# Edge coefficients of a graph kernel: from sixteen wide GpSimd operations to thirty-two narrow VectorE operations a tile

## The chip, the cores and the metric

The kernel runs on 1 core of one Trainium2 chip. The metric is the device time of one execution in microseconds; the profiled execution is one such run, with its trace.

## What is computed

A graph of 3125 nodes with 128 features and 103125 edges, sorted by destination. First comes a relational layer with 8 relations that share 4 bases, then two transformer layers over the same edges with 2 heads, each part with a residual and a norm:

```python
Hb = einsum('ni,bio->bno', h, V)            # 4 bases
coef = w_comp[etype]                        # (edges, 4)
m = sum_b coef[:, b] * Hb[b][src]           # then times norm (the edge weight)
agg = segment_sum(m, dst)
hn = relu(agg + h @ loop_w + bias)
y = hn @ ffn_w.T + ffn_b + h                # then layer norm, residual, norm
x = transformer_conv(relu(transformer_conv(x, ...)), ...)   # q, k, v, softmax over the edges of a node
```

The change is about `coef * norm`: for each edge, four numbers, each the sum over the 8 relations of (weight if the edge is of relation r, else 0) times `w_comp[r, b]`.

## The kernel before

`message` computes the relational layer in 25 tiles of 125 destination nodes; `conv`, called twice, computes the transformer layers over dense 125 x 3125 score tiles with an additive mask (`bias`) that `message` writes to memory.

In `message` each of the 128 partitions is a destination node with 64 edge slots. For tile s, GpSimd fetches the edge data (`find_row`, `find_slots`: indirect DMAs); VectorE makes `kinds` (L682, partition x 8 relations x 64 slots: the weight where the type is r, else 0) and `digits` in `slot_kinds`; the coefficients go to `codes` (4 bases x 2 copies x 64 slots); TensorE transposes `digits` (L832) and `codes` (L840) and ScalarE copies them out (`digitsT` L1011, `weightsT` L1023). VectorE then builds one-hot matrices in 8 units a tile (`build_hot`: `Hw` L735, `L` L737, `Hw` L740) in a ring of 4 buffers, TensorE multiplies them (L857, `pair_products`, side 0 is units 0 to 3, side 1 units 4 to 7), ScalarE copies the products out (`MT` L962), and TensorE sums them with the node features (L869, `sums`). Four times a tile TensorE also transposes counts (L880, `turn_counts`), ScalarE takes their logarithm (L989, `logs`), and VectorE turns that into the mask (L756, `bias_row`), which SyncE stores.

Each engine runs its own list of steps t, written out by hand, with semaphores between engines. At step t VectorE works on several tiles: `first(t-5)`, `second`, `third` (norms), `build_hot(t-3, 4..7)`, `search(t)`, `search_row(t-1)`, `bias_row(t-4, 0..3)`, `build_hot(t-2, 0..3)`, `slot_kinds(t-1)`. In `step` of VectorE the loop variable k runs over 8 slots: k = 0 holds `first` and the build of unit 4, k = 1 `search` and unit 5, k = 2 `second`, `search_row`, unit 6 and `bias_row(u, 0)`, k = 3 unit 7 and `bias_row(u, 1)`, `bias_row(u, 2)`, k = 7 `slot_kinds`. Three waits matter: the build of a unit waits until the unit whose buffer it takes is multiplied (L732, unit 4 waits for unit 0); `logs(u, 2)` waits for `bias_row(u, 0)` (L988, two buffers); and TensorE's `turn_counts(u, 3)` waits for `logs(u, 2)` (`read`, L886), `turn_codes` for `logs(u, 3)`, which waits for `bias_row(u, 1)`.

The coefficients are made on GpSimd in `coefs`, at the head of its step t for tile t-2: for each base one multiply of 512 columns by the broadcast coefficients (L577), then adds of 256, 128 and 128 columns (L578 to L580). For tile 0 alone VectorE makes three of the four bases (`first_tile`, L716 to L719), with `slot_kinds(0)` after the first of them. `root` (L558), the inverse square roots of the norms, is on GpSimd also.

At the head of each `conv`, TensorE projects q and k in 7 chunks of up to 500 columns (L1498, L1499) and ScalarE copies both out with their bias (L1611, L1614).

Of the kernel before, what the change touches and what calls it, by code (L numbers as in the profile page):

```python
# [16 lines left out]
F32 = mybir.dt.float32  # L17
# [13 lines left out]
SLOTS = 64  # L31
# [40 lines left out]
def is_int(t):  # L72
    return isinstance(t, int)
# [387 lines left out]
def message(nc, a, m):  # L461
# [5 lines left out]
    with ctx:  # L467
        def sb(name, shape, dt):
            return ctx.enter_context(nc.sbuf_tensor(name, shape, dt))

        def sem(name):
# [19 lines left out]
        part, part_v = sb("coef_parts", [128, RELS, SLOTS], F32), sb("coef_parts_v", [128, RELS, SLOTS], F32)  # L491
# [33 lines left out]
         asked2, rooted2, nrm1, nrm2, lifted, s3, kinds_ok, blank_ok, turned_ps, turned_ok, first_v, first_ok, first_kinds, digits_ps, digitsT_ok) = (  # L525
# [5 lines left out]
                "first_v", "first_ok", "first_kinds", "digits_ps", "digitsT_ok"))  # L531
# [19 lines left out]
        def _(pool):  # L551
# [9 lines left out]
            def coefs(s, par, halfway):  # L561

                first = is_int(s) and s == 0
                then = Steps(pool, gps, 0 if first else s * COEF_STEPS - (COEF_STEPS - FIRST_COEF_STEPS))
                to = codes[par]
                if is_int(s) and s == 0:
                    pool.wait_ge(m["comp_in"], 16)
                if not is_int(s) or s >= 2:
                    pool.wait_ge(codes_ps, s - 1)
                if first:  # L570
                    pool.wait_ge(first_kinds, 1)
                else:
                    pool.wait_ge(kinds_ok, s + 1)
                bases = BASES - FIRST_ON_V if first else BASES
                for b in range(bases):
                    c = comp[:, :].rearrange("p (r b) -> p b r", b=BASES)[:, b, :].unsqueeze(2).to_broadcast([128, RELS, SLOTS])
                    then(nc.gpsimd.tensor_tensor(part[:, :, :], kinds[:, :, :], c, ALU.mult))  # L577
                    then(nc.gpsimd.tensor_tensor(part[:, 0:4, :], part[:, 0:4, :], part[:, 4:8, :], ALU.add))  # L578
                    then(nc.gpsimd.tensor_tensor(part[:, 0:2, :], part[:, 0:2, :], part[:, 2:4, :], ALU.add))
                    last = nc.gpsimd.tensor_tensor(to[:, b, :, :], twice(part[:, 0, :]), twice(part[:, 1, :]), ALU.add)  # L580
                    if b < bases - 1:
                        then(last)
                    if b == 1:
                        halfway()
                last.then_inc(codes_ok, 1)
                pool.wait_ge(codes_ok, s + 1)

# [20 lines left out]
            def step(t, par):  # L608
                def first_root():
                    if inside(t - 5):  # L610
                        root(t - 5, 1 - par, 0)

                if inside(t - 2):
                    coefs(t - 2, par, first_root)
                else:
                    first_root()
                if inside(t - 5):
                    root(t - 5, 1 - par, 1)
                if inside(t - 4):
                    lift(t - 4, par)  # L620
                if inside(t) and (not is_int(t) or t >= EARLY):
                    if not is_int(t) or t >= 2:
                        pool.wait_ge(slot_ok, t - 1)
                    find_row(nc, pool, a, m, t, par)
                if is_int(t) and t == 1:
                    for s in range(EARLY):
                        find_slots(s, s)
                if inside(t - 1) and (not is_int(t) or t > EARLY):
                    find_slots(t - 1, 1 - par)
# [29 lines left out]
        def _(v):  # L659
# [25 lines left out]
            def slot_kinds(s, par):  # L685
# [5 lines left out]
                if not first:  # L691
                    v.wait_ge(kind_in[par], (half(s, par) + 1) * 32)
                V.tensor_scalar(off[:, :], e_dst[par][:, :], node[par][:, :], OWN, ALU.is_equal, ALU.mult)
# [11 lines left out]

            def first_tile():

                then = Steps(v, first_v)
                to = codes[0]
                v.wait_ge(kind_in[0], 32)  # L710
                kinds_of(0).then_inc(first_kinds, 1)
                v.wait_ge(m["comp_in"], 16)
                v.wait_ge(first_kinds, 1)
                for b in range(BASES - FIRST_ON_V, BASES):
                    c = comp[:, :].rearrange("p (r b) -> p b r", b=BASES)[:, b, :].unsqueeze(2).to_broadcast([128, RELS, SLOTS])
                    then(V.tensor_tensor(part_v[:, :, :], kinds[:, :, :], c, ALU.mult))  # L716
                    then(V.tensor_tensor(part_v[:, 0:4, :], part_v[:, 0:4, :], part_v[:, 4:8, :], ALU.add))
                    then(V.tensor_tensor(part_v[:, 0:2, :], part_v[:, 0:2, :], part_v[:, 2:4, :], ALU.add))
                    last = V.tensor_tensor(to[:, b, :, :], twice(part_v[:, 0, :]), twice(part_v[:, 1, :]), ALU.add)  # L719
                    if b < BASES - 1:  # L720
                        then(last)
                    if b == BASES - FIRST_ON_V:
                        slot_kinds(0, 0)
                last.then_inc(first_ok, 1)
# [101 lines left out]
        def _(pe):  # L826
# [8 lines left out]
            def turn_codes(s, par):  # L835
                pe.wait_ge(codes_ok, s + 1)
                if s == 0:
                    pe.wait_ge(first_ok, 1)
# [513 lines left out]
def conv(nc, a, m, layer, out):  # L1352
# [4 lines left out]
    with ctx:  # L1357
# [35 lines left out]
        names = ("dve", "q_ps", "q_ok", "k_ok", "v_ps", "v_ok", "qk", "masked", "neg_ok", "exp_ok", "t_ps", "pa_ok",  # L1393
# [13 lines left out]
        EXP_AT = 3  # L1407
        block = ctx.enter_context(nc.Block())
# [27 lines left out]
        def buffer_free(eng, u, i):  # L1436

            if not is_int(u) or u >= 1:
                eng.wait_ge(z["pv_ok"], (u - 1) * CH + (i // HEADS + 1))

# [49 lines left out]
        def _(pe):  # L1490
            pe.wait_ge(z["one"], 1)

            def project(j):

                if j >= 2:
                    pe.wait_ge(z["q_ok"], j - 1)
                    pe.wait_ge(z["k_ok"], j - 1)
# [24 lines left out]
            def scores(t, par, n):  # L1522
# [3 lines left out]
                if is_int(t) and t == 0:  # L1526
                    pe.wait_ge(z["k_ok"], j + 1)
# [258 lines left out]
```

## Time and profile before

| what | before |
|---|---|
| median of 3 runs | 1973.23 us (1972.51 to 1973.4) |
| profiled execution, device time | 1973.07 us |
| its span, first to last instruction | 1971.1 us |
| `message` in it | about 0 to 1057 us |
| TensorE, VectorE, ScalarE, GpSimd busy | 96%, 74%, 65%, 34% |
| mean granted TensorE clock | 0.994 |

The span plus 1.97 us around it is the device time. Times in timelines are microseconds from the start of the span. Busy time of an engine is the union of its instructions; where neighbouring instructions overlap in the pipeline, a row of x8 shows the union and not eight durations.

### The profile page before, as it was taken

The numbers are of one execution on the slowest core, as the hardware profiler recorded it, in microseconds if no ns is written. First come the engines' busy times: TensorE is split into PE (matmuls) and PEld (weight loads), VectorE is DVE, ScalarE is ACT, GpSimd is POOL, SyncE is SP. The second block draws the span as 40 slices with busy tenths as digits, with TensorE's granted clock in tenths as the row PEclk, the third lists the DMA queues.
The fourth block names the chain that finished last, engine by engine and source line by source line (L and its number), as shares of the span: only waits on it lengthen the run. The fifth ranks groups of instructions, "written<-read, shape, count | busy, mean of one in ns | idle before, by whom it ended". The sixth has DMA issues, their size and how long they took to land. (4 is left out here: it accounts for less than half of the span.)

```text
span 1971.1 us, 53480 instructions
## 1 busy us (share of the span) xinstructions
PE 1899.6 (96%) x19165; PEld 1647.1 (84%) x19165; DVE 1449.5 (74%) x4127; ACT 1281.2 (65%) x2289; POOL 673.3 (34%) x802
## 2 busy tenths in 40 slices
PE   1999999999999999999998999999999999999998
PEld 0889999999999999999995788888887788888887
DVE  5988878887888788778744777677663777777775
ACT  0757766777677767676764666666665666666665
POOL 3775676567656765676400000000000000000000
PEclk9999999999999999999998999999999999999999
DMA  3012111211111111111103222222211233222230
GB/s 78 15 49 70 41 41 50 70 41 41 52 68 41 41 54 66 40 41 53 60 35 131 101 100 97 80 85 96 97 65 66 101 107 106 98 93 92 103 105 11
DMA packets 43018, 137.00 MB, mean 70 GB/s; under 512 B 9190, under 2 KB 24359, under 8 KB 36484
## 3 DMA queue, kind: packets, MB, share of 16 engines
q1 hardware_dynamic: 38484, 128.24, 18.1%
q0 software_dynamic: 4400, 6.80, 1.5%
q8 instruction: 104, 1.70, 0.4%
q14 instruction: 30, 0.25, 0.0%
HBM read 91.83 MB, written 43.20 MB: 69 GB/s over the span
## 5 line engine op out<-in xcount | busy, mean ns | idle before, releaser
L869 PE MATMUL ps<-matrixT,x_rows 125*128 125x256 f32 (+1 forms) x2500 | 563.5, 377 | 0.1
L869 PEld LDWEIGHTS ps<-matrixT,x_rows 125*128 125x128 f32 x2500 | 461.3, 190 | 48.4 <-issue 0.2
L1729 DVE CUSTOM_DVE_ANT_0 scores_l<-ps,bias_rows_l 125x500 f32<-125x500 f32 (+1 forms) x700 | 390.0, 619 | 29.5 <-issue 28.6
L962 ACT COPY matrixT<-ps 125x500 f32<-125x500 f32 (+2 forms) x800 | 381.6, 659 | 38.4 <-PE ps L857 38.3
L857 PEld LDWEIGHTS ps<-high_weights,low_onehot 64*125 64x125 f32 x6300 | 355.0, 188 | 20.4 <-issue 17.2
L857 PE MATMUL ps<-high_weights,low_onehot 64*125 64x125 f32 x6300 | 364.9, 273 | 7.3 <-DVE high_weights L740 7.3
L1630 ACT ACTIVATE scores_l<-scores_l,neg_max_l 125x1500 f32<-125x1500 f32 x200 | 317.3, 1600 | 7.3 <-DVE neg_max_l L1750 7.3
L1518 PEld LDWEIGHTS ps<-weightsT_l,values_l 125*64 125x64 f32 x5000 | 267.8, 136 | 36.4 <-issue 34.1
L1559 PE MATMUL ps<-eye,scores_l 125*125 125x125 f32 x2500 | 295.2, 275 | 0.0
L1559 PEld LDWEIGHTS ps<-eye,scores_l 125*125 125x125 f32 x2500 | 281.1, 189 | 10.1 <-issue 9.5
L1541 PE MATMUL ps<-kT_l,q_tile_l 64*125 64x500 f32 (+1 forms) x1400 | 287.2, 547 | 1.7 <-issue 1.6
L1518 PE MATMUL ps<-weightsT_l,values_l 125*64 125x125 f32 x5000 | 279.7, 270 | 1.6 <-ACT hT L1658 1.6
L1638 ACT COPY weightsT_l<-ps 125x500 f32<-125x500 f32 x400 | 220.4, 577 | 91.9 <-PE ps L1559 86.9
L737 DVE TENSOR_TENSOR low_onehot<-own_low,digitsT 128x1000 f32<-128x1000 f32 x200 | 279.8, 1399 | 0.0
L1737 DVE COPY weightsT_l<-ps 125x500 f32<-125x500 f32 x200 | 135.1, 677 | 159.5 <-PE ps L1559 159.2
L1541 PEld LDWEIGHTS ps<-kT_l,q_tile_l 64*125 64x125 f32 x1400 | 144.0, 183 | 112.4 <-issue 77.5
L740 DVE TENSOR_TENSOR high_weights<-high_weights,edge_weightsT 128x800 f32<-128x800 f32 x200 | 223.4, 1117 | 0.0
L577 POOL TENSOR_TENSOR coef_parts<-kinds,comp 128x512 f32<-128x512 f32 x97 | 119.8, 1235 | 228.7 <-DVE digits L704 224.7
L989 ACT ACTIVATE ln<-ps,tiny 125x1000 f32<-125x1000 bf16 x100 | 95.7, 957 | 128.0 <-DVE bias L756 87.5
L1472 POOL COPY q_tile_l<-qT_l 128x125 f32 (+1 forms) x52 | 15.1, 291 | 436.8 <-PE ps L1541 403.1
L972 ACT CAST countsT<-matrixT 125x512 bf16<-125x512 f32 (+1 forms) x200 | 162.1, 953 | 0.0
L735 DVE TENSOR_TENSOR high_weights<-iota,digitsT 128x200 f32<-128x200 f32 x200 | 79.6, 398 | 98.9 <-PE ps L857 94.9
(152 smaller groups left out, 1609.3 us busy)
## 6 DMA issues: line engine op xcount, KB each, us to landing
bias_rows_l<-bias SPq DMA_DIRECT2D x50, 1562.5 KB, 6.7
bias<-bias SPq DMA_DIRECT2D x75, 500.0 KB, 2.9
x_rows<-in_x SPq DMA_DIRECT2D x1, 1562.5 KB
bias<-bias SPq DMA_DIRECT2D x25, 62.5 KB
x<-x_rows SPq DMA_DIRECT2D x25, 62.5 KB
x_rows_l<-x SPq DMA_DIRECT2D x25, 62.5 KB
out<-rows_l SPq DMA_DIRECT2D x25, 62.5 KB
dst_int<-in_dst SPq DMA_DIRECT2D x1, 402.8 KB
```

Of the source, the lines that this page charges most:

```text
L737: V.tensor_tensor(L[:, at, 0:p, :], own_low[:, :].unsqueeze(1).to_broadcast([128, p, R]), digitsT[par][:, 0, to].unsqueeze(2).to_broadcast ...
L740: V.tensor_tensor(Hw[:, at, 0:p, 0:BASES * T].rearrange("p n (h b) -> p n h b", b=BASES), hots.unsqueeze(3).to_broadcast([128, p, T, BASES ...
L857: last = nc.tensor.matmul(psP[2 * bank + q][0:R, 128 * (i % 4):128 * (i % 4) + COLS], L[own, at, i % GROUP, :], Hw[own, at, i % GROUP, 0:C ...
L869: last = nc.tensor.matmul(psG[:, BASES * SPLIT * side:BASES * (SPLIT * side + SIDE[side])], x[:, h, :], MT[side][:, 0:SIDE[side], BASES * ...
L962: last = nc.scalar.copy(MT[side][:, at:at + 2 * c - 1:2, 0:COLS], psP[2 * (g % 3) + q][0:R, :].rearrange("p (i c) -> p i c", c=128)[:, 0:c ...
L972: nc.scalar.copy(CT[:, lo:hi, SPLIT * side:SPLIT * side + SIDE[side]], MT[side][:, 0:SIDE[side], BASES * T + lo:BASES * T + hi].rearrange( ...
L1518: last = nc.tensor.matmul(psO[HD * hd:HD * (hd + 1), 0:R], vals[:, 4 * c + b, hd, :], weights, start=(c == 0 and b == 0), stop=(c == CH - ...
L1541: nc.tensor.matmul(score_bank(t, k)[0:R, 0:cw[j]], q_now[par][own, :], kT[own, CW * j:CW * j + cw[j]], start=True, stop=True).then_inc(z[" ...
L1559: last = nc.tensor.transpose(turn_bank(i)[0:R, at:at + R], S[up][:, hd, n * R:(n + 1) * R], eye[0:R, 0:R])
L1630: nc.scalar.activation(part, part, ACT.Exp, bias=neg[par][:, hd:hd + 1], accum_out=sums[par][:, hd, n // 2:n // 2 + 1]).then_inc(z["exp_ok ...
L1638: nc.scalar.copy(PT[i][:, 0:cw[c]], turn_bank(i)[0:R, 0:cw[c]]).then_inc(z["pa_ok"], 1)
L1729: V.tensor_tensor_reduce(S[par][:, hd, lo:hi], score_bank(t, HEADS * n + hd)[0:R, 0:cw[j]], bias[par][0:R, lo:hi], 1.0, FLOOR, ALU.add, AL ...
```

## The change

`coefs` leaves GpSimd. VectorE makes all coefficients, relation by relation: for each of the 8 relations four instructions, one a base, each with the coefficient as a per-partition scalar read from `comp`; seven relations of 64 columns, the last of 128 (it writes both copies). After each of the first seven relations VectorE waits for its own last instruction. The call stands in VectorE's step t at k = 0, after `first` and before the build of unit 4. The first tile is made in the same way, with `slot_kinds(0)` after all of it. `slot_kinds` gets one more wait, on an event of VectorE's own past. `root`, `lift` and the gathers stay on GpSimd, in the same order. In both `conv` layers the copies of the first four k chunks move from ScalarE to VectorE.

```diff
@@ message, GpSimd
-                bases = BASES - FIRST_ON_V if first else BASES
-                for b in range(bases):
-                    c = comp[:, :].rearrange("p (r b) -> p b r", b=BASES)[:, b, :].unsqueeze(2).to_broadcast([128, RELS, SLOTS])
-                    then(nc.gpsimd.tensor_tensor(part[:, :, :], kinds[:, :, :], c, ALU.mult))
-                    then(nc.gpsimd.tensor_tensor(part[:, 0:4, :], part[:, 0:4, :], part[:, 4:8, :], ALU.add))
-                    then(nc.gpsimd.tensor_tensor(part[:, 0:2, :], part[:, 0:2, :], part[:, 2:4, :], ALU.add))
-                    last = nc.gpsimd.tensor_tensor(to[:, b, :, :], twice(part[:, 0, :]), twice(part[:, 1, :]), ALU.add)
...
@@ message, VectorE
+            def coefs(s, par):
+                then = Steps(v, first_v, s * (RELS - 1))
+                to = codes[par]
...
+                for r in range(RELS):
+                    for b in range(BASES):
+                        by = comp[:, r * BASES + b:r * BASES + b + 1]
+                        if r == 0:
+                            last = V.tensor_scalar_mul(part[:, b, :], kinds[:, r, :], by)
+                        elif r < RELS - 1:
+                            last = V.scalar_tensor_tensor(part[:, b, :], kinds[:, r, :], by, part[:, b, :], ALU.mult, ALU.add)
+                        else:
+                            last = V.scalar_tensor_tensor(to[:, b, :, :], twice(kinds[:, r, :]), by, twice(part[:, b, :]), ALU.mult, ALU.add)
+                    if r < RELS - 1:
+                        then(last)
+                last.then_inc(codes_ok, 1)
...
             def first_tile():
...
                 kinds_of(0).then_inc(first_kinds, 1)
...
+                coefs(0, 0)
+                slot_kinds(0, 0)
...
@@ VectorE step
                     if k == 0 and inside(z):
                         first(z, 1 - par)
+                    if k == 0 and inside(t - 2) and (not is_int(t) or t > 2):
+                        coefs(t - 2, par)
...
@@ conv, ScalarE
+                if j < KEYS_V:
+                    continue
                 act.wait_ge(z["kk_ps"], j + 1)
@@ conv, VectorE (KEYS_V = 4)
+            for j in range(KEYS_V):
+                v.wait_ge(z["kk_ps"], j + 1)
+                V.tensor_scalar_add(kT[:, CW * j:CW * j + cw[j]], psQ[2 + j % 2][:, 0:cw[j]], bk[:, :]).then_inc(z["first_k_ok"], 1)
```

## Rows read from the trace of the kernel before

**Rows 1.** The page: busy time by engine, and the costliest group of `coefs`.
```profile
PE 1899.6 (96%) x19165; PEld 1647.1 (84%) x19165; DVE 1449.5 (74%) x4127; ACT 1281.2 (65%) x2289; POOL 673.3 (34%) x802
...
L577 POOL TENSOR_TENSOR coef_parts<-kinds,comp 128x512 f32<-128x512 f32 x97 | 119.8, 1235 | 228.7 <-DVE digits L704 224.7
```

**Rows 2.** Windows: us, then PE, PEld, DVE, ACT, POOL busy, clock, DMA, GB/s.
```profile
500.00:600.00 100.00, 100.00 (x994) 91.89 (x993) 81.78 (x163) 72.19 (x139) 61.53 (x64) 1.00 0.17 59
```

**Rows 3.** Timeline, TensorE: fourth count transpose of two tiles (start, length, engine, line).
```profile
816.45 0.22 PE L880 MATMUL ps<-eye,countsT 125*125 125x125 bf16 x1
...
855.74 0.22 PE L880 MATMUL ps<-eye,countsT 125*125 125x125 bf16 x1
```

**Rows 4.** Timeline, ScalarE: third logarithm of the same two tiles, idle before, releaser.
```profile
814.83 1.09 ACT L989 ACTIVATE ln<-ps,tiny 125x1000 f32<-125x1000 bf16 x1 [3.01 <-DVE bias L756]
...
854.29 1.09 ACT L989 ACTIVATE ln<-ps,tiny 125x1000 f32<-125x1000 bf16 x1 [3.17 <-DVE bias L756]
```

**Rows 5.** Timeline, VectorE, one steady step from `first` to `bias_row(u, 0)`.
```profile
836.73 0.15 DVE L764 TENSOR_SCALAR m_rstd<-m_mean 125x1 f32<-125x1 f32 x1
840.76 0.39 DVE L735 TENSOR_TENSOR high_weights<-iota,digitsT 128x200 f32<-128x200 f32 x1 [3.88 <-PE ps L857]
841.07 1.45 DVE L737 TENSOR_TENSOR low_onehot<-own_low,digitsT 128x1000 f32<-128x1000 f32 x1
...
843.60 0.14 DVE L228 COPY node<-ids 128x1 f32 x1
...
844.55 0.36 DVE L735 TENSOR_TENSOR high_weights<-iota,digitsT 128x200 f32<-128x200 f32 x1
...
848.22 0.35 DVE L779 SCALAR_TENSOR_TENSOR z_rows<-z_rows,m_rstd,x_shifted 125x128 f32<-125x128 f32 x1
...
853.01 1.19 DVE L756 SCALAR_TENSOR_TENSOR bias<-ln 125x1000 f32<-125x1000 f32 x1
```

**Rows 6.** Timeline, VectorE, a late step without search while GpSimd does no coefficients.
```profile
998.24 0.37 DVE L735 TENSOR_TENSOR high_weights<-iota,digitsT 128x200 f32<-128x200 f32 x1 [3.88 <-PE ps L857]
998.52 1.19 DVE L737 TENSOR_TENSOR low_onehot<-own_low,digitsT 128x1000 f32<-128x1000 f32 x1
...
1003.21 0.35 DVE L779 SCALAR_TENSOR_TENSOR z_rows<-z_rows,m_rstd,x_shifted 125x128 f32<-125x128 f32 x1
```

**Rows 7.** Source line L1685 (min/median/max ns), then a pair of it in the timeline.
```profile
L1685 DVE SCALAR_TENSOR_TENSOR rows_l<-ps,sum_l,skip_l x100: 274/280/285, 1110.4 to 1966.4; 125x64 f32<-125x64 f32 x100
...
1299.87 0.48 DVE L1685 SCALAR_TENSOR_TENSOR rows_l<-ps,sum_l,skip_l 125x64 f32<-125x64 f32 x2
```

**Rows 8.** Timeline, VectorE, `slot_kinds`: narrow operations with and without waits between.
```profile
513.97 0.25 DVE L693 TENSOR_SCALAR own_slots<-slot_dst,node 128x64 f32<-128x64 int32 x1
514.13 0.19 DVE L694 TENSOR_SCALAR slot_chunk<-slot_src 128x64 f32<-128x64 int32 x1
514.36 0.20 DVE L695 TENSOR_SCALAR slot_chunk<-slot_chunk 128x64 f32<-128x64 f32 x1
514.59 1.17 DVE L682 SCALAR_TENSOR_TENSOR kinds<-slot_type,slot_weight 128x64 f32<-128x64 int32 x8
```

**Rows 9.** Timeline of the start: VectorE, ScalarE's table load, and a TensorE wait.
```profile
30.90 1.17 DVE L682 SCALAR_TENSOR_TENSOR kinds<-slot_type,slot_weight 128x64 f32<-128x64 int32 x8 [7.10 <-DMA slot_weight<-in_edge_weight,slot_at]
...
38.24 1.28 ACT L1011 ACT_TABLE_LOAD   x1 [38.24 <-PE ps L832]
...
40.90 0.29 DVE L719 TENSOR_TENSOR codes<-coef_parts_v 128x128 f32<-128x128 f32 x1
...
42.46 0.74 ACT L1023 COPY edge_weightsT<-ps 64x252 f32<-64x252 f32 x2 [2.40 <-PE ps L840]
...
44.60 0.36 DVE L735 TENSOR_TENSOR high_weights<-iota,digitsT 128x200 f32<-128x200 f32 x1
...
104.49 0.27 PE L880 MATMUL ps<-eye,countsT 125*125 125x125 bf16 x1 [1.68 <-ACT ln L989]
```

**Rows 10.** Timeline, ScalarE, k copy at the head of the first `conv`.
```profile
1065.00 0.68 ACT L1614 ACTIVATE kT_l<-ps,bk 128x500 f32<-128x500 f32 x1 [0.16 <-PE ps L1499]
```

More of the change, by code:

```diff
@@ L490, in message @@
         kinds = sb("kinds", [128, RELS, SLOTS], F32)
-        part, part_v = sb("coef_parts", [128, RELS, SLOTS], F32), sb("coef_parts_v", [128, RELS, SLOTS], F32)
+        part = sb("coef_parts", [128, BASES, SLOTS], F32)
         codes = [sb(f"codes{i}", [128, BASES, 2, SLOTS], F32) for i in range(2)]
@@ L559, in root @@
                                         ALU.pow).then_inc(rooted, 1)
[L561 to L573, printed above, removed]
-                bases = BASES - FIRST_ON_V if first else BASES
-                for b in range(bases):
-                    c = comp[:, :].rearrange("p (r b) -> p b r", b=BASES)[:, b, :].unsqueeze(2).to_broadcast([128, RELS, SLOTS])
-                    then(nc.gpsimd.tensor_tensor(part[:, :, :], kinds[:, :, :], c, ALU.mult))
-                    then(nc.gpsimd.tensor_tensor(part[:, 0:4, :], part[:, 0:4, :], part[:, 4:8, :], ALU.add))
-                    then(nc.gpsimd.tensor_tensor(part[:, 0:2, :], part[:, 0:2, :], part[:, 2:4, :], ALU.add))
-                    last = nc.gpsimd.tensor_tensor(to[:, b, :, :], twice(part[:, 0, :]), twice(part[:, 1, :]), ALU.add)
[L581 to L586, printed above, removed]
             def find_slots(s, par):
@@ L608, in step @@
             def step(t, par):
[L609 to L616, printed above, removed]
+                if inside(t - 5):
+                    root(t - 5, 1 - par, 0)
                 if inside(t - 5):
@@ L704, in slot_kinds @@
                 V.tensor_tensor(to[:, 0, :, :], twice(low[:, :]), twice(off[:, :]), ALU.add).then_inc(kinds_ok, 1)
+            def coefs(s, par):
+                then = Steps(v, first_v, s * (RELS - 1))
+                to = codes[par]
+                if is_int(s) and s == 0:
+                    v.wait_ge(m["comp_in"], 16)
+                    v.wait_ge(first_kinds, 1)
+                else:
+                    v.wait_ge(kinds_ok, s + 1)
+                if not is_int(s) or s >= 2:
+                    v.wait_ge(codes_ps, s - 1)
+                for r in range(RELS):
[5 more added lines that the diff above has]
+                            last = V.scalar_tensor_tensor(part[:, b, :], kinds[:, r, :], by, part[:, b, :], ALU.mult, ALU.add)
+                        else:
+                            last = V.scalar_tensor_tensor(to[:, b, :, :], twice(kinds[:, r, :]), by, twice(part[:, b, :]), ALU.mult, ALU.add)
+                    if r < RELS - 1:
+                        then(last)
+                last.then_inc(codes_ok, 1)
@@ L706, in first_tile @@
             def first_tile():
-                then = Steps(v, first_v)
-                to = codes[0]
                 v.wait_ge(kind_in[0], 32)
                 kinds_of(0).then_inc(first_kinds, 1)
[L712 to L723, printed above, removed]
@@ L724, in first_tile @@
-                last.then_inc(first_ok, 1)
+                coefs(0, 0)
+                slot_kinds(0, 0)
             def build_hot(s, par, k):
@@ L1391, in conv @@
         spare, spare2 = sb("spare", [R, 1], F32), sb("spare2", [R, 1], F32)
-        names = ("dve", "q_ps", "q_ok", "k_ok", "v_ps", "v_ok", "qk", "masked", "neg_ok", "exp_ok", "t_ps", "pa_ok",
+        names = ("dve", "q_ps", "q_ok", "k_ok", "first_k_ok", "v_ps", "v_ok", "qk", "masked", "neg_ok", "exp_ok", "t_ps", "pa_ok",
                  "pv_ok", "pt", "rows_ok", "r_ps", "r_ok", "one", "fin_ok", "dve2", "asked",
@@ L1407, in conv @@
         EXP_AT = 3
+        KEYS_V = 4
         block = ctx.enter_context(nc.Block())
@@ L1439, in buffer_free, with keys_laid @@
                 eng.wait_ge(z["pv_ok"], (u - 1) * CH + (i // HEADS + 1))
+        def keys_laid(eng, n):
+            eng.wait_ge(z["first_k_ok"], min(n, KEYS_V))
+            if n > KEYS_V:
+                eng.wait_ge(z["k_ok"], n - KEYS_V)
         @block.sync
@@ L1526, in scores @@
                 if is_int(t) and t == 0:
-                    pe.wait_ge(z["k_ok"], j + 1)
+                    keys_laid(pe, j + 1)
                 if is_int(t) and t == 1 and n == 0:
```

9 lines of the change are left out of this document (4 added, 5 removed).

## The prediction

> **What bounds the kernel now.** I read the page first, then busy time by stretch, then the timelines of one steady step engine by engine. TensorE is busy 96% of the span, GpSimd 34% [rows 1], and in the steady part of `message` TensorE is busy all 100 of 100 us while VectorE has 82 and GpSimd 62 [rows 2]. So nothing taken off GpSimd or VectorE can shorten a steady step; it can only lengthen it, if TensorE begins to wait. The step is 855.74 - 816.45 = 39.29 us [rows 3], TensorE's own rate. The question is how near TensorE already is to waiting, and the nearest point is the fourth count transpose (L880). It needs the third logarithm, which ScalarE begins only when VectorE has done `bias_row(u, 0)`: it sat idle 3.01 and 3.17 us for that [rows 4]. The logarithms end at 815.92 and 855.38, the transposes start at 816.45 and 855.74 [rows 3, 4]: 0.53 and 0.36 us later. A few hundredths of that are the signal itself (I take 0.05), so the slack is 0.48 and 0.31 us, by turns, 0.40 in the mean. VectorE's 18% of idle time is elsewhere: from the release of unit 4 at 840.76 to the mask operation at 853.01 it works without a stop [rows 5].
>
> **What a tile's coefficients cost on VectorE.** The trace has no row for this exact form, so I build it. Nearest is L1685: 64 columns, a per-partition scalar, two tensors; one takes 0.280 us and a pair 0.48, so the second starts 0.20 after the first [rows 7]. Without a per-partition scalar, eight operations of 64 columns take 1.17 us, 0.136 apart [rows 8]; the scalar operand costs 0.06 each, in spacing as in duration. The one-tensor form with such a scalar (L693) lets its follower start 0.16 later and takes 0.25 [rows 8]. Where an operation needs the one before it, the follower starts 0.23 after the start of one that takes 0.19 [rows 8]: 0.04 for the wait. Hence: relation 0, 3 x 0.16 + 0.25 + 0.04 = 0.8; relations 1 to 6, each 3 x 0.20 + 0.28 + 0.04 = 0.92, together 5.5; relation 7 at 128 columns, the 64 more at 0.07 us (800 columns more take 1.19 - 0.37 = 0.82 us [rows 6]), 4 x 0.27 = 1.1. Sum 7.4 us. Bounds: at the spacing of the form without scalar, 7 x (3 x 0.136 + 0.22 + 0.04) + 4 x 0.21 = 5.5; with nothing overlapped, each at its whole duration, 28 x 0.28 + 4 x 0.35 + 7 x 0.04 = 9.5. I take 7.4, since L1685 is the same operation with the same operands but for PSUM as one source.
>
> The Trainium skill, page VectorE: DVE Perf Modes, section The DRAIN you can't avoid, says a semaphore after each operation costs nothing extra, since the next cannot start until the pipe is empty. The rows disagree: 0.136 apart without a wait against 0.23 with one [rows 8]. By the page the same 32 would come to about 6.7 us, and the loss below to some 14 us less.
>
> **Where they lie.** VectorE's `first` ends its last issue at 836.73, and its next instruction could start 0.07 later; it then waits until 840.76 for unit 0 to be multiplied, 4.03 us in all [rows 5]. The coefficients are put into that gap. They take 0.07 + 7.4 = 7.47, so unit 4 begins 7.47 - 4.03 = 3.44 us later than now. More than half is hidden by the old wait, the rest is not.
>
> **What comes back.** While GpSimd makes coefficients, VectorE's wide operations are stretched: the 1000-column build of unit 4 takes 1.45 us against 1.19 where GpSimd is idle [rows 5, 6]. From the start of unit 4 to L779 the step takes 848.22 - 840.76 = 7.46 [rows 5]. Without coefficients on GpSimd and without the search it takes 1003.21 - 998.24 = 4.97 [rows 6]; the search is 844.55 - 843.60 = 0.95 [rows 5]. So 7.46 - 5.92 = 1.54 us come back before `bias_row(u, 0)`. After L779 GpSimd does `root`, `lift` and `find_row` exactly as now, so that part does not change. More is regained behind it (unit 3 of the next tile), but there VectorE waits for TensorE anyway, and it is worth nothing.
>
> **A steady step.** `bias_row(u, 0)` ends 3.44 - 1.54 = 1.90 us later, less 0.40 slack: TensorE waits 1.5 us in each step, and `logs(u, 3)` follows with the same lateness, hidden behind the first wait. The wait is not made good: VectorE's `first` hangs on TensorE's own later work, so the ring VectorE, ScalarE, TensorE has a period of 39.3 + 1.5 = 40.8 us. Steps 5 to 24 have the full pattern: 20 x 1.5 = 30.0. Steps 25 and 26 have no search and more slack; between 0 and 3, I take 0.4.
>
> **The start.** For tile 0 VectorE begins after the kinds, which end at 32.07 [rows 9]. All four bases then take 7.4, to 39.6, against 41.19 now [rows 9]: 1.6 sooner. But `digits` of tile 0 used to go out in the middle and now come after; with 1.4 for `slot_kinds` without its kinds, at about 41.0; ScalarE's table load of 1.28, which now starts at 38.24 [rows 9], hangs on them and moves to about 41.7. With the copy behind it (0.5) the digits are out at 43.5, and the coefficients' transpose comes only then. From codes ready to weights copied takes 43.20 - 41.19 = 2.0, so unit 0 starts at about 45.5 and not 44.60 [rows 9]. In steps 3 and 4 the coefficients stand ahead of unit 4 with no gap to hide in; the uncontended builds pay back 5 to 6 of each 7.4. At the count transpose of 104.49, where TensorE already waits 1.68 [rows 9], and in the second wait behind it I count 2 us more than now. Bounds -1 and +4.
>
> **The k copies.** ScalarE waits 0.16 for TensorE before each k copy of 0.68 [rows 10]: TensorE sets the pace there, and VectorE has no work yet, as scores come later. The cover is TensorE's projections; worth 0, bounds -0.3 and +0.3 for both layers. The 16 GpSimd operations a tile (the widest 1.235 us [rows 1]) are worth nothing by themselves: their waits were for VectorE, not the reverse. The added wait in `slot_kinds` is for an event long past: 0 to 0.04 a step, off the tight stretch.
>
> **Sum.** 30.0 + 0.4 + 2.0 + 0 = 32.4 us on the profiled execution's 1973.07, whose distance to the median 1973.23 is nothing: 2005.5 us.
>
> **Rivals.** First, it is not slower: the scalar operand is free from SBUF (the 0.06 would belong to L1685's PSUM source). Then the coefficients take 5.5, unit 4 starts 1.54 later, the returned 1.54 cancels it, and slack swallows the rest. The decision point is 7.4 - 1.5 = 5.9 us for a tile's coefficients: below it no step gets longer. The start, with 1.9 us less in each of three blocks, ends about 3 us sooner than now: 1970 us, within 0.2% or just past it. For it speaks L682's spacing; against it L693, which has its scalar and its source in SBUF and still takes 0.06 more than L694 [rows 8].
>
> The Trainium skill, page VectorE: DVE Perf Modes, section on the TRN2 errata, gives an SBUF operation 58 cycles plus one a column at 0.96 GHz, and names no price for a scalar operand: 127 ns for 64 columns, an estimate of 4.3 us for all 32. That would end in this rival's case. The same section advises operands of at least 512 columns, which speaks against this change; L682's 136 ns agrees with its formula within a tenth.
>
> Second, the operations don't overlap, at 9.5 us: TensorE waits 3.6 a step and the time is 2005.5 + 20 x 2.1 = 2047. For it: in-place sums and a reused `part`; against: L1685's pair overlaps. Part of this case, say 8.4 us, gives 2026.
>
> **How the numbers follow.** Forecast 0.78, with its own range of 1997 to 2014 (a step's loss of 1.1 to 1.8 and the start's bounds); first rival 0.12, second 0.10. The range for 8 in 10 is 1994 to 2022: it reaches into both. A measurement of this kernel can tell about 0.2% (4 us) from no change. Slower by more than that: 0.78 + 0.10 - 0.02 = 0.86; within it 0.09; faster 0.05.
>
> **What would show it.** In the profile after: rows of the coefficients with pairs 0.20 apart, a block of about 7.4 us between L764's and unit 4's lines; unit 4 with no wait for TensorE; the builds of units 4 and 5 at 1.19 and not 1.45; TensorE idle before its fourth count transpose by about 1.5 us, released by ScalarE's logarithm; a step of 40.8 us; the conv layers as long as now. A block under 5.9 us, or a step of 39.3, makes the prediction wrong.

## The result, and the profile after

The kernel after takes 2004.34 us in the median of 4 runs (2003.13 to 2004.81), the kernel before 1972.87 in the 4 runs beside them: a ratio of 1.0164, with a 95% interval of 1.0152 to 1.0176. It is 31.5 us slower; 2005.5 was predicted. The profiled execution has a span of 2002.8 us, 31.7 more than the profiled one of before, and a mean granted clock of 0.995. What follows is about these 31.7 us.

The page first: busy time by engine, then a group of VectorE's work, the coefficients of relations 1 to 6 (busy time, mean ns of one | idle time before them).

```profile
PE 1904.6 (95%) x19165; PEld 1642.7 (82%) x19165; DVE 1540.0 (77%) x4923; ACT 1274.8 (64%) x2281; POOL 297.1 (15%) x414
...
L691 DVE SCALAR_TENSOR_TENSOR coef_parts<-kinds,comp,coef_parts 128x64 f32<-128x64 f32 x600 | 131.0, 281 | 5.3
```

GpSimd went from 34% [rows 1] to 15% and nobody gains by it. TensorE does the same 19165 matmuls and is busy 5.0 us longer, 0.3%, so its share fell because the span grew. The busy shares of the page don't tell why; the same stretch as in rows 2 does (windows: us, then PE, PEld, DVE, ACT, POOL busy, clock, DMA, GB/s):

```profile
500.00:600.00 100.00, 96.41 (x976) 88.08 (x974) 89.08 (x240) 66.63 (x128) 27.27 (x29) 1.00 0.13 46
```

TensorE, busy all 100 us before [rows 2], now stands idle for 3.59 of them, at full clock. VectorE is busy 89 us and still has 11 idle: it isn't full, it is late at one place. The waits of TensorE from 200 to 900 us name that place (line waited at and its releaser: us in total, times, longest):

```profile
PE ps L859 <- ACT ln L968: 21.2, 17, 1.4
```

It is the fourth count transpose (L880 before, L859 now), waiting 1.25 us in the mean for ScalarE's third logarithm, as in the argument on slack [rows 3, 4]. On TensorE's timeline, for two tiles:

```profile
844.25 0.27 PE L859 MATMUL ps<-eye,countsT 125*125 125x125 bf16 x1 [1.10 <-ACT ln L968]
...
885.26 0.27 PE L859 MATMUL ps<-eye,countsT 125*125 125x125 bf16 x1 [1.37 <-ACT ln L968]
```

The step was 39.29 [rows 3]; this one is 41.01, the one ahead of it, from 803.50, is 40.75, and they go on by turns, 40.88 in the mean.

The step grew by 1.59 us and the wait is 1.24 in the mean of the two. The other 0.35 are on TensorE itself. From the transpose to the pair products (the row of 124) it takes 2.81 us in the kernel before if the logarithm was done in time; it takes 3.00 if the logarithm ended only just ahead of the transpose, as at 541.21 (the logarithm ended at 541.15, and that step is 39.47 and not 39.29):

```profile
819.26 7.06 PE L857 MATMUL ps<-high_weights,low_onehot 64*125 64x125 f32 x124
...
541.21 0.27 PE L880 MATMUL ps<-eye,countsT 125*125 125x125 bf16 x1
...
544.21 7.06 PE L857 MATMUL ps<-high_weights,low_onehot 64*125 64x125 f32 x124
```

In the kernel after it takes 3.00 us in each steady step:

```profile
803.50 0.27 PE L859 MATMUL ps<-eye,countsT 125*125 125x125 bf16 x1 [1.38 <-ACT ln L968]
...
806.50 7.06 PE L836 MATMUL ps<-high_weights,low_onehot 64*125 64x125 f32 x124
```

So a step in which TensorE had to wait at all is 0.18 us longer for that, at full clock. The last 0.17 is how the trace counts: with no wait the transpose starts 0.17 us ahead of the modelled end of the matmuls before it (853.22 + 2.69 = 855.91 against 855.74). Why the 0.18 is lost, no run shows.

VectorE in the last of these steps shows the cause of the wait, to be read against rows 5:

```profile
863.83 0.29 DVE L749 TENSOR_TENSOR m_y_rows<-ps,x_raised 125x128 f32<-125x128 f32 x1 [2.71 <-PE ps L924]
...
864.89 0.77 DVE L689 TENSOR_SCALAR coef_parts<-kinds,comp 128x64 f32<-128x64 f32 x4
865.70 5.42 DVE L691 SCALAR_TENSOR_TENSOR coef_parts<-kinds,comp,coef_parts 128x64 f32<-128x64 f32 x24
871.15 1.14 DVE L693 SCALAR_TENSOR_TENSOR codes<-kinds,comp,coef_parts 128x128 f32<-128x128 f32 x4
872.21 0.36 DVE L714 TENSOR_TENSOR high_weights<-iota,digitsT 128x200 f32<-128x200 f32 x1
872.48 1.19 DVE L716 TENSOR_TENSOR low_onehot<-own_low,digitsT 128x1000 f32<-128x1000 f32 x1
...
878.12 0.35 DVE L758 SCALAR_TENSOR_TENSOR z_rows<-z_rows,m_rstd,x_shifted 125x128 f32<-125x128 f32 x1
...
882.83 1.19 DVE L735 SCALAR_TENSOR_TENSOR bias<-ln 125x1000 f32<-125x1000 f32 x1
```

From the start of L764 to that of unit 4 it was 4.03 us, 3.88 of them a wait for TensorE [rows 5]. In its place stand the coefficients, 872.21 - 864.89 = 7.32 us of them, and unit 4 (L714) starts right behind with no wait. The 1000-column build right behind takes 1.19 us and not 1.45 [rows 5].

### The profile page after: what moved, and what is told of

It reads as the page before. It is cut to its first block and busy times, and to the rows that moved or that the text cites. A ratio compares the mean times of both kernels' runs of the same rounds, so it can differ in the third digit from the quotient of the medians.

```text
span 2002.8 us, 53742 instructions
## 1 busy us (share of the span) xinstructions
PE 1904.6 (95%) x19165; PEld 1642.7 (82%) x19165; DVE 1540.0 (77%) x4923; ACT 1274.8 (64%) x2281; POOL 297.1 (15%) x414
## 5 line engine op out<-in xcount | busy, mean ns | idle before, releaser
L716 DVE TENSOR_TENSOR low_onehot<-own_low,digitsT 128x1000 f32<-128x1000 f32 x200 | 238.4, 1192 | 0.0
L719 DVE TENSOR_TENSOR high_weights<-high_weights,edge_weightsT 128x800 f32<-128x800 f32 x200 | 194.8, 974 | 0.0
L1609 ACT COPY sumsT_l<-ps 128x125 f32<-128x125 f32 x50 | 13.2, 264 | 201.0 <-PE ps L1504 201.0
L558 POOL TENSOR_TENSOR m_rstd<-m_rstd,minus_half_m 125x1 f32<-125x1 f32 x50 | 29.1, 581 | 723.6 <-DVE m_rstd L743 723.6
L691 DVE SCALAR_TENSOR_TENSOR coef_parts<-kinds,comp,coef_parts 128x64 f32<-128x64 f32 x600 | 131.0, 281 | 5.3
```

Of the source, the lines that this page charges most:

```text
L716: V.tensor_tensor(L[:, at, 0:p, :], own_low[:, :].unsqueeze(1).to_broadcast([128, p, R]), digitsT[par][:, 0, to].unsqueeze(2).to_broadcast ...
L719: V.tensor_tensor(Hw[:, at, 0:p, 0:BASES * T].rearrange("p n (h b) -> p n h b", b=BASES), hots.unsqueeze(3).to_broadcast([128, p, T, BASES ...
```

## Experiments

Each ratio is against runs of the kernel before on the same chip. A time without a ratio is of a single run. The step is always from one fourth count transpose to the next. Two theories stand against each other at first. The first is that of the prediction: the length of VectorE's block of coefficients, where it stands, sets the loss, since it is longer than the gap plus what the faster builds return. The rival is that something other than its length costs time: the scalar operands themselves, GpSimd's lost work, or a part of the change elsewhere.

### Where the block stands: ahead of `first`

```diff
 for k in range(UNITS):
+    if k == 0 and inside(t - 2) and (not is_int(t) or t > 2):
+        coefs(t - 2, par)
     if k == 0 and inside(z):
         first(z, 1 - par)
-    if k == 0 and inside(t - 2) and (not is_int(t) or t > 2):
-        coefs(t - 2, par)
```

> Edit: the changed kernel with the coefficients called before `first` and not after it; the same 32 operations. Theory (the ring through `first`, the block, units 4 to 6, the mask and the logarithm): part of the block of 7.3 us now lies in VectorE's wait of 2.7 us for TensorE ahead of `first`, the rest pushes `first` 4.6 us, of which the old wait of 3.95 behind it takes all but 0.65; 1.5 us of faster builds cover that. Step 39.3 us, TensorE without a wait at the fourth count transpose, time 1972 to 1975. Rival (VectorE has simply too much work, or small operations on VectorE disturb others): the step stays near 40.9 and the time near 2004.

Measured: 1971.57 us, ratio 0.9999 (0.9989 to 1.0009). The step is 39.29 to 39.30. VectorE's timeline of one step:

```profile
518.01 0.73 DVE L689 TENSOR_SCALAR coef_parts<-kinds,comp 128x64 f32<-128x64 f32 x4
518.78 5.42 DVE L691 SCALAR_TENSOR_TENSOR coef_parts<-kinds,comp,coef_parts 128x64 f32<-128x64 f32 x24
...
525.29 0.28 DVE L749 TENSOR_TENSOR m_y_rows<-ps,x_raised 125x128 f32<-125x128 f32 x1
...
526.27 0.37 DVE L714 TENSOR_TENSOR high_weights<-iota,digitsT 128x200 f32<-128x200 f32 x1
```

The same 32 operations take the same 7.28 us. But ahead of `first` VectorE had a second gap, which the kernel before shows in the same step as rows 5:

```profile
835.85 0.29 DVE L770 TENSOR_TENSOR m_y_rows<-ps,x_raised 125x128 f32<-125x128 f32 x1 [1.35 <-PE ps L945]
```

Put ahead of both gaps, the block has 1.35 + 4.03 us of waiting to fill, 1.54 that the builds return and 0.40 of slack, 7.32 us, and more: the build of unit 3, ahead of `first`, was stretched too. In the kernel before, its 1000 and 800 columns take 2.05 and 1.51 us, here 1.19 and 0.98, 1.39 less (before):

```profile
831.01 2.05 DVE L737 TENSOR_TENSOR low_onehot<-own_low,digitsT 128x1000 f32<-128x1000 f32 x1
```

That is 8.7 us for a block of 7.28. `first` starts right behind it without a wait, unit 4 as well, and the third logarithm waits for TensorE and no more for the mask; it ends 1.24 us ahead of the transpose at 540.74 (ScalarE, this kernel):

```profile
538.41 1.09 ACT L968 ACTIVATE ln<-ps,tiny 125x1000 f32<-125x1000 bf16 x1 [2.30 <-PE ps L859]
```

No step is longer, and the time is 0.4 us below the expected range. The k copies and the added wait in `slot_kinds` are in this kernel too. So all the loss in the steady steps hangs on the place of the block. Its work as such, on an engine with idle time left, costs nothing.

### The other end of the chain: masks earlier

```diff
+    if k == 2 and inside(u):
+        bias_row(u, 0)
+    if k == 3 and inside(u):
+        bias_row(u, 1)
     build_hot(w, 1 - par, k + AHEAD)
-    if k == 2 and inside(u):
-        bias_row(u, 0)
     if k == 3 and inside(u):
-        bias_row(u, 1)
         bias_row(u, 2)
```

> Edit: the changed kernel with bias_row(u, 0) before the build of unit 6 and bias_row(u, 1) before that of unit 7, the coefficients where they are. Theory: the logarithms that TensorE waits for start 2.3 us and more sooner, more than the 1.5 us lost; units 6 and 7 come 1.1 and 2.3 us later, with several us to spare. Step 39.3 us, time 1972 to 1976. If the late builds (and not the mask) are what holds TensorE, the step stays 40.9 or grows.

Measured: 1969.87 us, ratio 0.9989 (0.9979 to 0.9998), a step of 39.29. The step is as expected, the time 2 us under the range. 1.3 us are gained in the start: the fourth count transpose of the second tile stands at 146.35 us, at 147.61 in the kernel before and 149.25 in the one after. The window of 500 to 600 us:

```profile
500.00:600.00 100.00, 100.00 (x994) 92.15 (x994) 89.62 (x236) 71.06 (x138) 31.85 (x29) 1.00 0.16 54
```

Here the block stands exactly where the change put it and is as long (7.28 to 7.32 us). Only `bias_row(u, 0)` no longer stands behind the build of unit 6, nor `bias_row(u, 1)` behind that of unit 7. VectorE is busy 89.62 of 100 us and TensorE all 100: VectorE's share is even above that of the kernel after, where TensorE waits. What counts is not how much VectorE does but what stands between the block and the mask that ScalarE's third logarithm needs.

### The price of the scalar operand: constants

```diff
-        by = comp[:, r * BASES + b:r * BASES + b + 1]
+        by = 0.25 + 0.125 * (r * BASES + b)
```

The coefficients of the bases are replaced by constants; the output is another.

> Edit: the changed kernel with constants in the instructions in place of the per-partition coefficients, so the coefficients are not those of the reference. Theory: each of the 32 operations loses 0.06 us of spacing, the block goes from 7.3 to 5.4 us, below the 5.8 at which steps stop growing: step 39.3 us, time about 1972. If the scalar operand costs nothing in this place: block 7.3, step 40.9, 2004.

Measured: 1967.10 us, a step of 39.29. The block of this kernel on VectorE's timeline:

```profile
517.61 0.50 DVE L689 TENSOR_SCALAR coef_parts<-kinds 128x64 f32<-128x64 f32 x4
518.14 3.96 DVE L691 SCALAR_TENSOR_TENSOR coef_parts<-kinds,coef_parts 128x64 f32<-128x64 f32 x24
522.13 0.90 DVE L693 SCALAR_TENSOR_TENSOR codes<-kinds,coef_parts 128x128 f32<-128x128 f32 x4
522.95 0.36 DVE L714 TENSOR_TENSOR high_weights<-iota,digitsT 128x200 f32<-128x200 f32 x1
```

The same number of operations, columns and waits takes 5.34 us, not 7.32. One operation of relations 1 to 6 has a median of 219 ns, against 281 ns in the kernel after: 0.06 us for an operand that is a scalar for each partition in SBUF. So the price read off L1685 [rows 7] belongs to the operand and not to PSUM. The block is then below the 5.9 us that the prediction named as the point of decision, and no step is longer. The first rival would have been true if this price had been nothing, and it would have ended here. It ended 3 us below its 1970 and 5 below what was expected of this run, and that is in the start: the fourth count transpose of the second tile stands at 143.26 us instead of 147.61, and that of 541.21 at 536.44.

### The length of the block: one relation less, and two

```diff
-        for r in range(RELS):
+        for r in (0, 1, 2, 3, 4, 5, 7):
```

Relation 6 is left out of the coefficients, and with it one of the seven waits (its line isn't shown). In the second kernel relations 5 and 6 are left out, `(0, 1, 2, 3, 4, 7)`.

> Edit: the changed kernel with relation 6 left out of the coefficients (28 operations and six waits in place of 32 and seven). Theory: the block is 0.90 us shorter and above the point of decision, so every step gains all of it: step 40.88 - 0.90 = 39.98 us, time about 1985. If the wait at the transpose had another cause, the step moves by less than half of 0.9.

> Edit: the changed kernel with relations 5 and 6 left out of the coefficients (24 operations and five waits). Theory: the block is 7.3 - 1.8 = 5.5 us, below the point of decision at 5.8, so only part of the second relation's 0.9 counts: step 39.3 us and not 39.1, TensorE without a wait; time 1968 to 1971. If there is no such point and every 0.9 counts in full or not at all: step 39.1 or 40.0.

Measured: 1985.01 us with seven relations; the block takes 6.38 and 6.60 by turns, the steps are 39.85 and 40.32, 40.10 in the mean. That is the expected 1985 and 39.98. With six the time is 1966.65 us, a block of 5.47 and a step of 39.29 to 39.30: the expected step, and a time 1.4 us under the range, again by the start (that of the second tile at 142.53). On TensorE's timeline the wait with seven relations is down to 0.69 us, and 0.24 in the other step:

```profile
546.60 0.27 PE L859 MATMUL ps<-eye,countsT 125*125 125x125 bf16 x1 [0.69 <-ACT ln L968]
```

With six there is no wait, and slack is left: the logarithms end 0.60 and 0.35 us ahead of the transposes, by turns. Here it is 535.34 and 535.70 (ScalarE, then TensorE):

```profile
534.25 1.09 ACT L968 ACTIVATE ln<-ps,tiny 125x1000 f32<-125x1000 bf16 x1 [3.18 <-DVE bias L735]
...
535.70 0.22 PE L859 MATMUL ps<-eye,countsT 125*125 125x125 bf16 x1
```

### The waits between relations

In the change all four bases of one relation are followed by a wait for the last of them. Here each operation waits only for its own base's sum of the relation before, which is four operations back.

```diff
-    then = Steps(v, first_v, s * (RELS - 1))
+    done = s * (RELS - 1) * BASES
     ...
+            if r > 0:
+                v.wait_ge(first_v, done + (r - 1) * BASES + b + 1)
     ...
-        if r < RELS - 1:
-            then(last)
+            if r < RELS - 1:
+                last.then_inc(first_v, 1)
```

> Edit: the changed kernel with each operation of a relation waiting only for its own partial sum of the relation before, four operations back, and not all four for the last one. Theory: the wait for the last operation exposes 0.12 us (0.28 + 0.04 - 0.20) seven times, so the block goes from 7.3 to 6.5 us, still above the point of decision: step 40.88 - 0.8 = 40.1 us, time about 1986. If a wait between two VectorE operations costs nothing: step 40.9, 2004; if each of the 28 added waits costs something itself, slower than that.

Measured: 1982.93 us; the block takes 6.40 to 6.44, the steps are 39.87 and 40.14, 40.01 in the mean. The 6.5 and 40.1 expected were nearly right, the time is 3 us lower. VectorE's timeline:

```profile
526.12 0.74 DVE L691 TENSOR_SCALAR coef_parts<-kinds,comp 128x64 f32<-128x64 f32 x4
526.77 4.78 DVE L693 SCALAR_TENSOR_TENSOR coef_parts<-kinds,comp,coef_parts 128x64 f32<-128x64 f32 x24
531.47 1.14 DVE L695 SCALAR_TENSOR_TENSOR codes<-kinds,comp,coef_parts 128x128 f32<-128x128 f32 x4
532.52 0.37 DVE L716 TENSOR_TENSOR high_weights<-iota,digitsT 128x200 f32<-128x200 f32 x1
```

There are four times as many waits, and the block is 0.88 us shorter; the 24 operations start (531.47 - 526.77) / 24 = 0.196 us apart. A wait as such doesn't cost; one that holds a narrow operation back until the one just before it is done does. Seven of these cost 0.13 each; rows 7 and 8 give 0.12, the overlap lost (0.28 - 0.20 = 0.08) and 0.04. The Trainium skill, page VectorE: DVE Perf Modes, section The DRAIN you can't avoid, says that a semaphore after each of eight copies costs nothing extra, and that leaving them out gains nothing. For operations this narrow the trace doesn't agree: the signals are free here as well, the wait on the operation just before is not.

Five lengths of the block in the same place now stand against their steps:

| block, us | step, us |
|---|---|
| 7.30 | 40.88 |
| 6.50 (one relation less) | 40.10 |
| 6.42 (waits spread) | 40.01 |
| 5.47 (two relations less) | 39.29 |
| 5.34 (constants) | 39.29 |

From 7.30 to 6.42 the step falls by 0.87 for 0.88 of block, one for one. Drawn on, the line meets 39.29 at 7.30 - 1.59 = 5.7 us, and the two blocks below that are on the floor. But the knee isn't at 5.7. Read from below, the block of 5.47 leaves 0.60 and 0.35 us between logarithm and transpose, less 0.05 for the signal: 0.43 in the mean, and 5.47 + 0.43 = 5.90. The constants leave 0.73 and 0.48, and 5.34 + 0.56 = 5.90 again. From there the steps come out with the 0.18 us that a step with a wait takes longer: 39.29 + 0.18 + (7.30 - 5.90) = 40.87, and 40.07 and 39.99 for the blocks of 6.50 and 6.42, where 40.88, 40.10 and 40.01 were measured. A knee at 5.9 with a slope of one is the prediction's model, and at the knee there is a small jump that it didn't have. No theory in which each operation or its operand costs by itself gives a knee.

### GpSimd's old work beside the new

To the kernel after, GpSimd's 16 old operations a tile are added again, on buffers of their own, at the head of its step. Their results aren't used.

```diff
+    def idle_coefs(s, halfway):
+        then = Steps(pool, gps, (s - 1) * 16 + 1)
+        ...
+        for b in range(BASES):
+            c = comp[:, :].rearrange("p (r b) -> p b r", b=BASES)[:, b, :].unsqueeze(2).to_broadcast([128, RELS, SLOTS])
+            then(nc.gpsimd.tensor_tensor(part_p[:, :, :], kinds_p[:, :, :], c, ALU.mult))
+            then(nc.gpsimd.tensor_tensor(part_p[:, 0:4, :], part_p[:, 0:4, :], part_p[:, 4:8, :], ALU.add))
+            then(nc.gpsimd.tensor_tensor(part_p[:, 0:2, :], part_p[:, 0:2, :], part_p[:, 2:4, :], ALU.add))
+            then(nc.gpsimd.tensor_tensor(codes_p[:, :, :], twice(part_p[:, 0, :]), twice(part_p[:, 1, :]), ALU.add))
```

> Edit: the changed kernel, in which GpSimd also does its old sixteen coefficient operations a tile, at their old place, on buffers of its own that nobody reads. Theory (the 1.54 us that came back per step were the stretching of VectorE's builds by GpSimd): they are lost again, step 40.9 + 1.5 = 42.4 us, more if GpSimd also stretches the narrow coefficient operations; time 2035 or above. If the builds got faster for another reason: step 40.9, time 2004 (GpSimd itself has time to spare).

Measured: 2144.47 us, at a mean granted clock of 0.964, with steps of 45.8 to 47.5 us, 46.7 in the mean. The direction is as expected; the size (42.4 us and more) and the place are not. VectorE's timeline of one step:

```profile
516.73 1.12 DVE L711 TENSOR_SCALAR coef_parts<-kinds,comp 128x64 f32<-128x64 f32 x4
517.88 8.52 DVE L713 SCALAR_TENSOR_TENSOR coef_parts<-kinds,comp,coef_parts 128x64 f32<-128x64 f32 x24
...
527.50 0.36 DVE L736 TENSOR_TENSOR high_weights<-iota,digitsT 128x200 f32<-128x200 f32 x1
527.77 1.20 DVE L738 TENSOR_TENSOR low_onehot<-own_low,digitsT 128x1000 f32<-128x1000 f32 x1
```

GpSimd's last coefficient operation in that step:

```profile
524.71 0.51 POOL L574 TENSOR_TENSOR codes_p<-coef_parts_p 128x128 f32<-128x128 f32 x1
```

That is over before the block ends at 527.50, so the build of unit 4 isn't stretched at all (1.20). The stretching fell on the block itself, 10.77 us instead of 7.32 (10.3 to 10.9 in other steps), and on the build of unit 3 ahead of it, where GpSimd's first operations lie: its 1000 columns take 2.06 us at 510.82 and 1.19 without GpSimd's work. Nothing but GpSimd's work was added, so it does slow VectorE's two-tensor operations, as the prediction had it from 1.45 against 1.19 [rows 5, 6]. How much of the 1.54 us that came back in the kernel after would be lost with the same overlap as before, this kernel doesn't tell, since the overlap is another one.

The step grew by 46.7 - 40.9 = 5.8 us. The wait at the transpose grew by 3.6 of them, from 1.24 to 4.82 us in the mean. The other 2.2 us are on TensorE behind the wait. Its timeline in two steps, then a window of 2 us, in which the column behind the five busy times is the granted clock:

```profile
493.65 4.38 PE L870 MATMUL ps<-matrixT,x_rows 125*128 125x244 f32 x10
...
540.62 0.36 PE L881 MATMUL ps<-eye,countsT 125*125 125x125 bf16 x1 [4.90 <-ACT ln L990]
...
541.00 3.65 PE L870 MATMUL ps<-matrixT,x_rows 125*128 125x244 f32 x10
```

```profile
540.00:542.00 2.00, 1.38 (x6) 1.24 (x7) 2.00 (x3) 1.09 (x3) 1.70 (x2) 0.59 0.64 256
```

After 4.7 to 4.9 us of idling the granted clock is near one half, the 1.2 GHz level, for some 3.5 to 5 us (0.56 from 542 to 544, 1.00 from 544; 0.50 from 493 to 499), and ten sums take 3.65 or 4.38 us that take 2.28 at full clock (the before kernel at 104.71 us has them at 2.28). From the transpose to the end of the pair products a step loses 1.4 to 2.8 us by it.

### The k copies alone

The kernel before, with nothing of the change but that the first four k copies of each `conv` layer are VectorE's:

```diff
...
+            for j in range(KEYS_V):
+                v.wait_ge(z["kk_ps"], j + 1)
+                V.tensor_scalar_add(kT[:, CW * j:CW * j + cw[j]], psQ[2 + j % 2][:, 0:cw[j]], bk[:, :]).then_inc(z["first_k_ok"], 1)
...
```

> Edit: the kernel before with only the second part of the change, the first four k copies of each conv layer on VectorE. Theory: TensorE sets the pace of the projections, so no change: 1972 to 1973.5. If ScalarE's copies had held TensorE, up to 2 us faster in each layer.

Measured: 1972.27 us against 1970.91, ratio 1.0004 (0.9995 to 1.0013), no difference that the runs can tell. One copy takes 0.74 us on VectorE against 0.68 on ScalarE [rows 10], and waits for TensorE either way (in the kernel after):

```profile
1096.69 0.74 DVE L1656 TENSOR_SCALAR kT_l<-ps,bk 128x500 f32<-128x500 f32 x1 [0.94 <-PE ps L1485]
```

### Everything moved into gaps

Coefficients ahead of `first`, masks early, waits spread as above, and in the first tile the digits ahead of the coefficients:

```diff
...
 def first_tile():
     ...
-    coefs(0, 0)
     slot_kinds(0, 0)
+    coefs(0, 0)
```

> Edit: the changed kernel with all of it: coefficients before `first`, masks 0 and 1 before units 6 and 7, spread waits, and for the first tile the digits before the coefficients. Theory: steps of 39.3 us as TensorE allows, and 1 us less at the first unit and 0.8 in each of three blocks of the start than with early masks alone (1969.9): 1966 to 1968, faster than both. If TensorE's rate is all that counts and the start does not matter: 1969 to 1972.

Measured: 1965.53 us in 7 runs, ratio 0.9973 (0.9962 to 0.9984). It is faster than both kernels: by 5.4 us than the one before, and so by some 37 than the one after, each against runs of before on its own chip. The steady step is 39.29, the same as before. Most of the gain lies in the start. The fourth count transpose that stands at 541.21 us in the kernel before comes at

```profile
536.09 0.22 PE L862 MATMUL ps<-eye,countsT 125*125 125x125 bf16 x1
```

and that of the first tile, at 104.49 before [rows 9], at 101.86; that of the second, at 147.61 before, at 142.92. So 4.7 us are gained by the second tile, and 0.4 more by 541 us, where some steps of the kernel before have its logarithm only just in time and take 39.5. Which of the four edits brings how much, this run doesn't tell; masks early alone brought a ratio of 0.9989. In the steady steps TensorE's own rate is the floor, and moving work off GpSimd doesn't touch it.

## Why the prediction was right, step by step

**The bound and the slack.** TensorE at 39.29 us a step, 0.40 us from waiting at its fourth count transpose: now the transpose at 885.26 follows the logarithm (884.12, 1.09 us) by 0.05, the price taken for the signal, and waits in each steady step. The slack can't be read off the kernel after, but its sum with gap and return can be read off the shorter blocks: a knee at 5.90, as predicted. The 0.48 and 0.31 by turns hold for most steps of the kernel before and not for all: at 265.96 and 541.21 the logarithm ends 0.06 us ahead of the transpose, so nothing is left there. What the model lacked is the 0.18 us of a step in which TensorE waits.

**The block.** Predicted 0.8 + 5.5 + 1.1 = 7.4 us; measured 0.81 + 5.45 + 1.06 = 7.32 (starts 864.89, 865.70, 871.15 and 872.21). L1685 was the right nearest row, though its source is in PSUM: 281 ns against its 280. The bounds were both real forms: 5.5 was to be had with constants (5.34); the 9.5 of no overlap was not approached. The Trainium skill, page VectorE: DVE Perf Modes, section on the TRN2 errata, has 58 cycles plus one a column, from which 4.3 us is an estimate; the trace doesn't agree for this form, whose narrow operations take 281 ns, start 196 ns apart where no wait stands between, and not 127.

**Where it lies.** Unit 4 starts 7.37 or 7.50 us after the start of `first`'s last operation (831.33 - 823.96, 872.21 - 864.71), instead of 4.03: 3.34 to 3.47 later; predicted 3.44.

**What comes back.** From unit 4 to L758 it takes 878.12 - 872.21 = 5.91 us; predicted 5.92, before 7.46 [rows 5]. The 1.54 us came back to a hundredth, 1.37 on the builds of units 4 and 5 and the rest on the operation behind them. That GpSimd's operations had stretched them is shown by the run with its old work beside the new, for unit 3's build; for these two it is the same reading.

**A steady step.** Predicted 40.8, measured 40.88, by two small errors that meet: by the predicted knee the measured block of 7.30 gives 1.40 us and not 1.5, and each wait costs 0.18 besides. The twenty steps, from `first` to `first` (VectorE, before, then after):

```profile
128.52 0.15 DVE L764 TENSOR_SCALAR m_rstd<-m_mean 125x1 f32<-125x1 f32 x1
...
915.31 0.15 DVE L764 TENSOR_SCALAR m_rstd<-m_mean 125x1 f32<-125x1 f32 x1
```

```profile
128.95 0.15 DVE L743 TENSOR_SCALAR m_rstd<-m_mean 125x1 f32<-125x1 f32 x1
...
946.47 0.15 DVE L743 TENSOR_SCALAR m_rstd<-m_mean 125x1 f32<-125x1 f32 x1
```

They took 786.79 us and take 817.52: 30.7 more, where 30.0 was predicted. Steps 25 and 26 add 0.42 (predicted 0.4).

**The start: the term that was mis-sized.** Predicted +2.0, measured 128.95 - 128.52 = +0.43. Two things in it went another way. Unit 0 began at 44.90 and not 45.5: the kinds' first operation started at 30.16 instead of 30.90 [rows 9], since their DMA landed 0.74 us sooner in this execution. And at the count transpose the 2 us more did come (106.97 against 104.49), but not what was to follow:

```profile
106.97 0.27 PE L859 MATMUL ps<-eye,countsT 125*125 125x125 bf16 x1 [3.52 <-ACT ln L968]
...
107.19 3.96 PE L848 MATMUL ps<-matrixT,x_rows 125*128 125x244 f32 x10
110.99 0.60 PE L819 MATMUL ps<-eye,codes 128*128 128x128 f32 x4
111.52 7.14 PE L836 MATMUL ps<-high_weights,low_onehot 64*125 64x125 f32 x124
```

The kernel before at the same place:

```profile
104.71 2.28 PE L869 MATMUL ps<-matrixT,x_rows 125*128 125x244 f32 x10
108.97 0.66 PE L840 MATMUL ps<-eye,codes 128*128 128x128 f32 x4 [1.99 <-ACT ln L989]
109.56 8.67 PE L857 MATMUL ps<-high_weights,low_onehot 64*125 64x125 f32 x124
```

Before, TensorE waits twice, 1.68 [rows 9] and 1.99 us, and then does the pair products at a lowered clock (0.50 in the window of 110 to 112), 8.67 us instead of 7.14. After, the one wait of 3.52 us lowers the clock at once (0.50 in 108 to 110), and it falls on the ten sums, 3.96 instead of 2.28, behind which it would have had to wait again. So the second wait is gone and the pair products run at full clock: 2.0 us behind at the codes' transpose, 0.4 behind at the end of the products (118.66 - 118.23). The prediction counted waits and left out that the clock was lowered already in the kernel before. That the lowered clock costs nothing where a wait would have followed is argued from these rows, and no run was made for it alone.

**The conv layers.** `message` gives way to `conv` at 1089.08 instead of 1057.49 us, 31.6 later; what comes after is 0.1 us longer, with the k copies in it. Predicted 0, and the run with these alone says the same.

**Sum.** 0.4 + 30.7 + 0.4 + 0.1 = 31.6 us of the 31.7, against 2.0 + 30.0 + 0.4 + 0 = 32.4. Two errors of 1.6 and 0.7 partly cancel: the total is nearer than the start deserved.

**The rivals.** The first, no loss because the scalar operand is free, had its point of decision right (5.9) and its premise wrong (0.06 us for each operation). Its 1970 us would have been 1967.1. The second, no overlap, didn't come up: 0.20 us from one start to the next where no wait stands between.

## What to carry to other kernels

Before work is moved to an engine with idle time, look where on its timeline the idle time lies, and what stands behind the moved block on the way to the engine that sets the pace: the same 7.3 us a step cost 31 us in one gap and nothing one gap earlier, or with two masks moved ahead of two builds. Price narrow operations by a row with the same kinds of operands, since the operand's kind (0.28 against 0.22 us, 2.0 us a block) and the distance between dependent operations (0.9 us a block) are each more than half of the 1.4 us by which the block was too long here. Where the pacing engine is at its own rate in the steady part, the gain of such a move is to be had mostly in the start, 4.7 of 5.4 us here.

## What the runs showed of the hardware that was not expected

- GpSimd's operations on SBUF stretch narrow VectorE operations too: the block went from 7.3 to 10.8 us (by 47%). The 1000-column operation goes from 1.19 to 1.45 us in rows 5 (by 22%) and to 2.06 (by 73%) where it meets the first of GpSimd's operations.
- TensorE's clock doesn't fall for waits of 1.1 to 1.4 us once a step (1.00 granted from 500 to 600 us in the kernel after), but to its lower level, 1.2 GHz, after waits of 3.5 and 4.9 us, and in the kernel before after two of 1.68 and 1.99 us close together. A late mask therefore costs more than its lateness once it is late enough: of 5.8 us a step in the kernel with GpSimd's old work, 2.2 were clock.
- A step in which TensorE waits at all takes 0.18 us more than its wait, even where the wait is too short to show (39.47 us from 541.21 in the kernel before, at full clock).
- Of 28 waits a block on an operation four places back none shows, while seven on the operation just before cost 0.9 us.
